# Attention plus gated feed-forward on eight cores: leaving the running maximum and its rescaling out of the softmax

## The reference

```python
def attn(x, W_spin, b_spin, W_global, W_J, beta):
    s = einsum('bni,oi->bno', x, W_spin) + b_spin
    g = einsum('bmd,od->bmo', mean(s, axis=1, keepdims=True), W_global)
    e = einsum('bnd,od->bno', s, W_J)
    scores = einsum('bnd,bmd->bnm', e, s) / sqrt(1024)
    local = einsum('bnm,bmd->bnd', softmax(scores, axis=-1), s)
    return tanh(beta * (s + g + local))

def ffn(x, w_gate, w_up, w_down):      # int weights, times 1/127
    return einsum('bsh,dh->bsd', silu(gate) * up, wd)

x = x + layernorm(attn(layernorm(x), ...))
x = x + layernorm(ffn(layernorm(x), ...))
```

## Time and profile before

| | |
|---|---|
| times of two runs | 1406.51 and 1563.26 us, median 1484.88 |
| profiled execution, its own time | 1399.61 us |
| span of its slowest core (7) | 1398.1 us |
| spans of its eight cores | 1380.4 to 1398.1 us |
| TensorE busy on core 7 | 1188.1 us, 85% |
| VectorE, ScalarE, GpSimd busy | 494.7, 220.8, 72.9 us |

### The profile page before, as it was taken

The page is one execution under the profiler, slowest core; times in us unless marked ns, Lnnn a source line. Parts: engine busy times, 40 slices in busy tenths (PEclk is TensorE's granted clock), DMA queues, the critical chain, the costliest instruction groups (busy, mean ns, idle before and its releaser), DMA issues.

```text
span 1398.1 us, 14919 instructions; the slowest of 8 cores (1380.4 to 1398.1 us)
## 1 busy us (share of the span) xinstructions
PE 1188.1 (85%) x5274; PEld 512.8 (37%) x5274; DVE 494.7 (35%) x860; ACT 220.8 (16%) x359; POOL 72.9 (5%) x92
## 2 busy tenths in 40 slices
PE   0798887867999999999999402599999999999997
PEld 0233332223444444444444100244444444444443
DVE  2243433302334443444344278411212121233443
ACT  0111111211112221222222110111111111100000
POOL 0011110000000000000000100001111111000000
PEclk9999998999999999999999755799999999999999
DMA  9755665771122232232222399834645537123322
GB/s 192 155 114 136 148 130 138 157 125 33 38 53 53 61 61 53 52 59 64 53 46 52 84 252 314 179 37 42 79 46 66 56 30 91 16 91 96 116 90 90
DMA packets 230393, 131.04 MB, mean 94 GB/s; under 512 B 204720, under 2 KB 204720, under 8 KB 230320
## 3 DMA queue, kind: packets, MB, share of 16 engines
q1 hardware_dynamic: 83488, 67.16, 19.2%
q0 software_dynamic: 57744, 29.37, 15.8%
q10 hardware_dynamic: 89088, 33.57, 11.2%
HBM read 92.31 MB, written 25.17 MB: 84 GB/s over the span
## 4 chain that ended last, share of the span: by engine, by line
PE 76%; DMA 10%; DVE 7%; issue 3%; ACT 2%; ACTq 1%; DVEq 0%; SPq 0%
PE ps_pv L716 16%; PE ps_q L548 12%; PE ps_d L1146 12%; PE ps_u L1053 12%; PE ps_g L1042 12%; PE ps_s L256 7%; DMA xnT_sb<-xn_bf 5%; PE ps_e L305 3%; DMA x_sc<-x_buf 2%; DVE qm L567 2%; DMA xs<-x 1%; PE ps_s L252 1%; PE ps_pv L432 1%; DVE x_buf L889 1%; DMA xn2T<-xn_bf 1%
## 5 line engine op out<-in xcount | busy, mean ns | idle before, releaser
L1042 PE MATMUL ps_g<-xn2T,wg_sb 128*128 128x512 bf16 x768 | 176.9, 389 | 94.1 <-DMA xn2T<-xn_bf 94.1
L716 PE MATMUL ps_pv<-s_tok,PT_sb 128*128 128x512 bf16 x1024 | 228.1, 384 | 10.6 <-DVE PT_sb L679 9.7
L548 PE MATMUL ps_q<-s_FM,ebuf 128*128 128x512 bf16 x1024 | 225.4, 381 | 8.7 <-DMA ebuf<-e_sc 8.7
L1053 PE MATMUL ps_u<-xn2T,wu_sb 128*128 128x512 bf16 x768 | 169.8, 379 | 0.0
L1146 PE MATMUL ps_d<-wdT_sb,h_act 128*128 128x512 bf16 x768 | 165.9, 379 | 1.0 <-DVE h_act L1076 1.0
L1076 DVE SCALAR_TENSOR_TENSOR h_act<-silu_b,ps_u 128x512 bf16<-128x512 f32 x96 | 66.1, 688 | 266.9 <-PE ps_u L1053 265.9
L716 PEld LDWEIGHTS ps_pv<-s_tok,PT_sb 128*128 128x128 bf16 x1024 | 100.2, 99 | 138.3 <-issue 23.9
L548 PEld LDWEIGHTS ps_q<-s_FM,ebuf 128*128 128x128 bf16 x1024 | 100.1, 98 | 131.5 <-issue 12.4
L1042 PEld LDWEIGHTS ps_g<-xn2T,wg_sb 128*128 128x128 bf16 x768 | 76.2, 100 | 190.6 <-issue 103.8
L256 PE MATMUL ps_s<-wspT_sb,xnT_sb 128*128 128x512 bf16 x512 | 137.7, 417 | 0.0
L1146 PEld LDWEIGHTS ps_d<-wdT_sb,h_act 128*128 128x128 bf16 x768 | 75.1, 98 | 91.9 <-issue 1.5
(11 more groups left out here) (74 smaller groups left out, 498.8 us busy)
## 6 DMA issues: line engine op xcount, KB each, us to landing
xs<-x SPq DMA_DIRECT2D x24, 1024.0 KB, 6.6
x_sc<-x_buf ACTq DMA_DIRECT2D x16, 512.0 KB, 6.1
xs<-x_sc SPq DMA_DIRECT2D x16, 512.0 KB, 4.6
out<-out_b SPq DMA_DIRECT2D x16, 512.0 KB, 5.5
wg_sb<-wgT POOLq DMA_DIRECT2D x24, 256.0 KB, 4.4
wu_sb<-wuT POOLq DMA_DIRECT2D x24, 256.0 KB, 5.4
wdT_sb<-wdT POOLq DMA_DIRECT2D x4, 1536.0 KB, 14.8
e_sc<-e_stage POOLq DMA_DIRECT2D x32, 128.0 KB, 2.4
```

The lines of the kernel that those rows point to most:

```text
L548: i = t.matmul(ps_q[:, slot, half * 512:(half + 1) * 512], ebuf[:, qt % 2, j, :], s_FM[:, j, qi * 1024 + half * 512: qi * 1024 + (half + 1 ...
L716: i = t.matmul(ps_pv2[:, nb * 512:(nb + 1) * 512], PT_sb[:, par, cb * P:(cb + 1) * P], s_tok[:, cb, nb * 512:(nb + 1) * 512], start=(cb == ...
L1042: i = t.matmul(ps_g[:, tb, :], wg_sb[:, par, j, :], xn2T[:, j, tb * 512:(tb + 1) * 512], start=(j == 0), stop=(j == KC - 1))
L1053: i = t.matmul(ps_u[:, tb, :], wu_sb[:, par, j, :], xn2T[:, j, tb * 512:(tb + 1) * 512], start=(j == 0), stop=(j == KC - 1))
```

## The change

The exponential no longer subtracts a maximum. `c_fvq` is gone, with its 64 maxima over 1,024 scores and 64 biases; `fvc`, `fcf` and `fvre` are gone too, so `PT_sb` is used as the DMA wrote it. `fvr` keeps the sum of the four row sums and its inverse, and waits for the last exponential of its tile. The exponential waits for TensorE instead of VectorE, and has the constant 0.0 as its bias. Each group of 16 matmuls of `P s` waits for its DMA transpose instead of VectorE's rescaling, and the first of a tile also for `fv4` of the tile before, which read the same `ps_pv`; that was implied before. Five small buffers go. The softmax itself is the same in exact arithmetic.

```diff
-        def c_fvq(qt, qi):
...
-            def fvq(v, qt=qt, qi=qi, slot=slot, cp=cp):
-                v.wait_ge(st.h, rec[("scq", qt, qi)])
-                if qi == 0 and qt >= 1:
-                    v.wait_ge(ss.h, rec[("expq", qt - 1, 3)])
-                i = v.reduce_max(out=qm4[:, cp, qi:qi + 1],
-                                 in_=ps_q[:, slot, :], axis=AX.X)
-                vinc(sv, i)
-                v.wait_ge(sv.h, sv.n)
-                i = v.tensor_scalar_mul(out=biasq[:, cp, qi:qi + 1],
-                                        in0=qm4[:, cp, qi:qi + 1],
-                                        scalar1=-INV32)
-                vinc(sv, i)
...
             def fexp(s, qt=qt, qi=qi, slot=slot, cp=cp,
-                     wv=rec[("qmaxb", qt, qi)],
+                     wt=rec[("scq", qt, qi)],
                      wtr=rec.get(("ptr", qt - 1, qi), 0),
                      wrs=rec.get(("rsfix", qt - 1), 0)):
-                s.wait_ge(sv.h, wv)
+                s.wait_ge(st.h, wt)
...
-                             bias=biasq[:, cp, qi:qi + 1], scale=c_inv32[:],
+                             bias=0.0, scale=c_inv32[:],
...
         def c_quarter(qt, qi):
             c_scq(qt, qi)
-            c_fvq(qt, qi)
             c_fexp(qt, qi)
             c_fptr(qt, qi)
...
-            def fvc(v, qt=qt, cp=cp, wcf=rec.get(("cfac", qt - 2), 0)):
...
-            def fcf(s, qt=qt, cp=cp, wv=rec[("dcol", qt)]):
...
             if qt + 1 < NT_OWN:
                 c_scq(qt + 1, 0)
 
-            for bq in range(4):
-                def fvre(v, qt=qt, bq=bq, par=par, cp=cp):
...
-                    i = v.tensor_scalar(
-                        out=PT_sb[:, par, bq * 1024:(bq + 1) * 1024],
-                        in0=PT_sb[:, par, bq * 1024:(bq + 1) * 1024],
-                        scalar1=cfac[:, cp, bq:bq + 1], scalar2=None,
-                        op0=ALU.mult)
...
             def fvr(v, qt=qt, cp=cp):
-                i = v.tensor_tensor(out=rsq[:, cp, :], in0=rsq[:, cp, :],
-                                    in1=cfac[:, cp, :], op=ALU.mult)
-                vinc(sv, i)
-                v.wait_ge(sv.h, sv.n)
+                v.wait_ge(ss.h, rec[("expq", qt, 3)])
                 i = v.reduce_sum(out=rstot[:, cp, :], in_=rsq[:, cp, :],
                                  axis=AX.X)
...
-            if qt + 1 < NT_OWN:
-                c_fvq(qt + 1, 0)
...
                 def ftv(t, qt=qt, bq=bq, par=par, sv_gbc=sv_gbc):
-                    t.wait_ge(sv.h, rec[("resc", qt, bq)])
+                    w = rec[("ptr", qt, bq)]
+                    t.wait_ge(w[0].h, w[1])
+                    if bq == 0 and qt >= 1:
+                        t.wait_ge(sv.h, rec[("stt", qt - 1)])
                     if qt == 0 and bq == 0:
                         t.wait_ge(sv.h, sv_gbc)
```

More of the change, by code:

```diff
@@ L385, in build_program @@
         PT_sb = eC(nc.sbuf_tensor("PT_sb", [P, 2, N], BF16))
[L386 to L390, removed]
         rsq = eC(nc.sbuf_tensor("rsq", [P, 2, 4], F32))
@@ L556, in c_scq @@
             rec[("scq", qt, qi)] = st.n
-        def c_fvq(qt, qi):
-            qg = 4 * qt + qi
-            slot = qg % 3
-            cp = qt % 2
-            def fvq(v, qt=qt, qi=qi, slot=slot, cp=cp):
-                v.wait_ge(st.h, rec[("scq", qt, qi)])
-                if qi == 0 and qt >= 1:
-                    v.wait_ge(ss.h, rec[("expq", qt - 1, 3)])
-                i = v.reduce_max(out=qm4[:, cp, qi:qi + 1],
-                                 in_=ps_q[:, slot, :], axis=AX.X)
-                vinc(sv, i)
-                v.wait_ge(sv.h, sv.n)
-                i = v.tensor_scalar_mul(out=biasq[:, cp, qi:qi + 1],
-                                        in0=qm4[:, cp, qi:qi + 1],
-                                        scalar1=-INV32)
-                vinc(sv, i)
-            block.vector(fvq)
-            rec[("qmaxb", qt, qi)] = sv.n
         def c_fexp(qt, qi):
@@ L645, in build_program @@
                 e_load(qt + 2)
-            def fvc(v, qt=qt, cp=cp, wcf=rec.get(("cfac", qt - 2), 0)):
[L648 to L651, removed]
-                vinc(sv, i)
-                v.wait_ge(sv.h, sv.n)
[L654 to L660, removed]
-            def fcf(s, qt=qt, cp=cp, wv=rec[("dcol", qt)]):
[L663 to L668, removed]
             if qt + 1 < NT_OWN:
                 c_scq(qt + 1, 0)
-            for bq in range(4):
-                def fvre(v, qt=qt, bq=bq, par=par, cp=cp):
[L675 to L678, removed]
-                    i = v.tensor_scalar(
-                        out=PT_sb[:, par, bq * 1024:(bq + 1) * 1024],
-                        in0=PT_sb[:, par, bq * 1024:(bq + 1) * 1024],
-                        scalar1=cfac[:, cp, bq:bq + 1], scalar2=None,
-                        op0=ALU.mult)
-                    vinc(sv, i)
-                block.vector(fvre)
-                rec[("resc", qt, bq)] = sv.n
             def fvr(v, qt=qt, cp=cp):
-                i = v.tensor_tensor(out=rsq[:, cp, :], in0=rsq[:, cp, :],
-                                    in1=cfac[:, cp, :], op=ALU.mult)
-                vinc(sv, i)
-                v.wait_ge(sv.h, sv.n)
+                v.wait_ge(ss.h, rec[("expq", qt, 3)])
                 i = v.reduce_sum(out=rstot[:, cp, :], in_=rsq[:, cp, :],
```

## The result

| | before | changed |
|---|---|---|
| median of the runs | 1405.22 us (10 runs) | 1384.13 us (11 runs) |
| ratio, with its 95% interval | | 0.9852 (0.9831 to 0.9873) |
| profiled execution | 1399.61 us | 1381.44 us |
| span of the slowest core | 1398.1 us (core 7) | 1379.9 us (core 1) |
| VectorE busy on that core | 494.7 us | 373.0 us |

The median of before is over more runs than were shown ahead of the prediction. The runs of 1563, 1580 and 1584 us, in the last two of which the cores of one die show a mean granted clock of 0.80 to 0.82 instead of 0.95, are left out of the ratio. The kernel is 1.5% faster, 21 us. The interval is clear of 1, but the gain is less than the 2% from which a difference counts here as "faster". Forecast was 1.65%.

What follows compares the result with a forecast made beforehand. TensorE, busy 85% of the span, was taken as the bound. Steady tiles 8.1, tile 15 6.9 and tile 0 8.2 sum to 23.2 us, giving 1376.4 and 1383.3 from two runs, middle 1380; range 1366 to 1394 with run variation.

Steps and rivals of the forecast that it cites:

- Steady tiles: Tiles 1 to 14: the 0.58 us wait of `P s` for VectorE's rescaling goes 14 times, 8.1 us.
- nothing comes late in its place: Tiles 1 to 15: transposes and exponentials stay hidden behind the score pass, cost 0; 5.6 us to spare even in tile 15.
- Tile 15: Before the last `P s`, 4.03 us of idle time go, and 2.85 us of slower clock behind it: 6.9 us.
- Tile 0: Waits for global-term copies and the clock behind them: 2.90 + 1.67 + 1.96 + 1.69 = 8.2 us.
- 2.90: Tile 0: piece 2's wait for the mean's copy, behind the quarter-3 maximum, goes; 2.90 us.
- 1.67: Tile 0: piece 3's 16 matmuls take 3.63 us instead of 5.30 as the clock no longer falls; 1.67 us.
- 1.96: Tile 0, piece 4: of the second half's 2.86 us wait for the first half's copy, 1.96 us go.
- The last part: Tile 0: the first `P s` takes 13.97 us instead of 15.66 as the clock stays up; 1.69 us, other end 0.
- the clock terms stay: Rival: gaps left in tile 0 still drop the clock, or it rises slowly; gain 17, time 1386, chance 0.15.
- VectorE's reads of `ps_q`: Rival: removing 64 reads that slow TensorE wins at most 5 us more; time 1372, chance of more than 2% 0.16.
- granted less in a denser attention: Rival: without short pauses TensorE gets less clock in attention; with six slow passes 1463, chance 0.03.
- peak-current limiter: Skill's rule: dense matmuls on three or more cores bring the die to 13/16 clock; attention 107 us more.

Runs made afterwards that it cites:

- e5: Changed kernel, with the first group of `P s` in tile 15 made to wait for the DMA transpose of quarter 3; 1396.03 us.
- e1: Kernel before, keeping each quarter's maximum and bias but without common maximum, factors and rescaling of `PT_sb` and row sums; 1394.83 us, ratio 0.9854 to before.
- e3: Changed kernel, with the halves of piece 4 in two banks of `ps_pv`, issued between the halves of score quarter (1,0); 1387.45 us.
- e4: Changed kernel, with the first group of `P s` in tile 15 made to wait for the exponential of quarter 3; 1390.39 us.
- e2: Kernel before, nothing removed, with VectorE's copies of the mean and global term moved earlier in tile 0; 1403.85 us, ratio 0.9953 to before.

## Why the prediction was right

**Steady tiles**: 8.1 us forecast; the second kind of pass is now 13.81 instead of 14.39 us apart, 14 times, 8.1. The argument that nothing comes late in its place held: on no core does `P s` wait for a transpose or a pass of scores for ScalarE.

**Tile 15**: 6.9 forecast; 4.03 and 2.84 measured between core 7 before and the rows above. Over the eight cores the second part is smaller: before, the pass took 15.3 to 15.4 us on three of them and 16.7 to 16.9 on five, 16.2 on average, so 2.3 us were won. e5 shows that the second part was the clock. e1 has both terms without the rest of the change: over the eight cores 8.0, 4.0 and 2.3, with 0.8 in piece 4 and 0.9 in the first `P s`, make its 16.0.

**Tile 0**: 8.2 forecast. The parts 2.90 and 1.67 came as forecast (5.30 became 3.61), and the 2.86 became 0.94, 1.92 for 1.96. The 1.67 holds for seven cores of eight, and over the eight the part is 1.5: on core 1 of before the clock had not fallen behind the same 2.90 us.

```profile
329.65 0.33 PE L451 MATMUL ps_pv<-ones_col,mf_bf 1*128 1x1 bf16 x8 [2.90 <-DVE mf_bf L442]
330.52 3.61 PE L470 MATMUL ps_pv<-wglT_sb,mfT_bf 128*1 128x512 bf16 x16 [0.53 <-DVE mfT_bf L460]
```

Between the cast of the product and the copy of `g_bc` the trace of before has 11 instructions of VectorE, not 14, and two are left; the 1.96 us don't hang on that count.

The last part, 1.69 for the clock in the first `P s`, is the term that was mis-sized. The prediction took all of it, because 1.69 us of idle time in the projection had not let the clock fall. It came back on three of eight cores, and on five, the slowest among them, the pass still took 15.7 us or close to it. That is 0.7 on average and 0 on the slowest core. One pause of 1.69 us was the wrong row to go by for two pauses of 0.94 us with a single one-row matmul between. e3 takes the pauses away and gets the 1.69 on all cores.

**The sum** was 23.2, and 21.0 was measured in attention. From start to start, over the eight cores: 8.0 in the steady tiles, 4.0 and 2.3 in tile 15, and 3.0, 1.5, 2.0 and 0.7 in tile 0 make 21.5. Of the missing 2.2 us some 1.0 is the mis-sized term, 0.6 the clock in tile 15, 0.2 that in piece 3. The other 0.5 stand in no term: the first 32 score matmuls, which start at the lower clock behind the wait for `ebuf`, took 8.8 us on average in the profile of before and 9.2 in this one. No part of the change touches them, and in the profiles that keep that wait the mean lies between 8.6 and 9.2. The forecast time, 1380, was 4 us low: 2 are the smaller gain, and 2 that it was counted from 1403, where the median of before came to 1405.2.

**The rivals.** That the clock terms stay came true for one of the three, and on part of the cores. VectorE's reads of `ps_q` do not slow TensorE: a pass is 13.81 us with them and without. The clock was not granted less in a denser attention: 1.00 from 400 to 740 us on all eight cores. The rule of the Trainium skill (TensorE: Matmul & The Clock Gate, Part 1) on the peak-current limiter would have brought it to 13/16; the trace doesn't show that, so the small chance that the prediction gave it was right for the executions compared here.

## What to carry to other kernels

Price removed work by what the bottleneck engine waited for, from start to start, and look at what stands ahead of the awaited instruction in its queue: here 122 us of VectorE work were worth 21 us, and 5.7 were to be had by moving three copies up in VectorE's queue. A pause of TensorE has a second price where the clock falls behind it: here 1.7 us behind one of 2.90, and 1.3 to 3.0 behind one of 3.87. Whoever removes pauses should remove the small ones next to each other too, and take the price over all cores, as it differs between them for the same pause.

## What the runs showed of the hardware

A bias given as a column of SBUF costs an exponential of 128x1024 from PSUM 89 ns against the constant 0.0 (1204 and 1115 ns). The Trainium skill (ScalarE: Activation LUTs, What ACT_TABLE_LOAD costs) gives some 93 ns for such an operand; these rows agree.

Whether the clock falls behind a pause isn't decided by that pause's length alone: behind two of 0.94 us it fell on five cores of eight in the changed kernel and on 37 of 48 over the six profiles with that tile 0 (8 of 8 in e4, 5 of 8 at the least), behind one of 1.50 us on none of eight (e4), behind 2.13 and 0.94 us on three of eight (e1). Behind 2.90 us it fell on 14 of 16 (before and e1), behind 3.87 on 16 of 16 (before and e2). In the changed kernel the cores run the same instructions with the same pauses there, so one core's row is not enough to say what such a pause costs.

In the second norm the two cores of a pair (0 and 1, 2 and 3, and so on) are not alike. From `fv4` of tile 15 to the first gate matmul, the core of each pair whose attention ends first, counted from each core's own first instruction, took 45.4 to 45.8 us in the changed kernel, and the other, 4 to 7 us later, 49.8 to 55.5. Before it was 44.7 to 47.0 and 47.8 to 52.7. That the two share what this DMA-bound stage needs is the likely reason, but no run here took it apart. The slowest core of both kernels is one that came late, so the time can move a little more or less than attention does.
